# Two-layer kernel: the experts of layer 1 on plain fp32 matmuls, their product moved from VectorE to GpSimd

## What is computed

```python
logits = einsum('bsd,ed->bse', xn, gate_w)            # 16 experts
topk_w, topk_idx = top_k(softmax(logits).transpose, cap)   # cap = 512 tokens per expert and batch
x_tok = take(xn, topk_idx)
g = einsum('becd,efd->becf', x_tok, Wg)               # 256 -> 512
u = einsum('becd,efd->becf', x_tok, Wu)
h = gelu(g) * u
eo = einsum('becf,edf->becd', h, Wd) * topk_w         # 512 -> 256, scattered back and added
out = scatter_add(eo) + shared_expert(xn)             # the same three products, for every token
```

## Time and profile before

| | us |
|---|---|
| runs | 4758.56, 4765.51, 4766.25 |
| median | 4765.51 |
| span of the profiled execution | 4756.4 |
| PE busy | 4083.1 (86%) |
| DVE busy | 3477.4 (73%) |
| POOL busy | 2589.5 (54%) |
| ACT busy | 2579.2 (54%) |

### The profile page before, as it was taken

One profiled execution on the slowest core, in us unless ns is written; L12 is line 12 of the kernel. 1 busy time (PEld: TensorE's weight loads), 2 busy tenths in 40 slices (PEclk: granted clock), 3 DMA queues, 4 the chain that ended last, 5 costly groups with the idle time before them and its releaser, 6 DMA issues. The chain is left out here.

```text
span 4756.4 us, 68001 instructions
## 1 busy us (share of the span) xinstructions
PE 4083.1 (86%) x24660; PEld 3380.9 (71%) x24660; DVE 3477.4 (73%) x4975; ACT 2579.2 (54%) x4869; POOL 2589.5 (54%) x1858
## 2 busy tenths in 40 slices
PE   8899999979999999978888866778888887888865
PEld 7788888858788888867777755656676666666653
DVE  5466666655566666626888889988888888888887
ACT  6544444437444444447576653256667666666655
POOL 3122222223122210026666656878999899999887
PEclk9999999989999999979999967889999999999996
DMA  2022222221122210024444431255655556556658
GB/s 90 19 97 76 85 86 76 88 87 41 52 89 73 88 58 20 22 68 141 148 143 140 141 112 60 81 173 167 192 178 179 176 186 188 173 172 190 188 164 315
DMA packets 271490, 572.90 MB, mean 120 GB/s; under 512 B 37169, under 2 KB 157746, under 8 KB 271154
## 3 DMA queue, kind: packets, MB, share of 16 engines
q1 hardware_dynamic: 246578, 534.98, 33.7%
q0 software_dynamic: 24576, 33.57, 3.9%
HBM read 445.64 MB, written 122.81 MB: 120 GB/s over the span
## 5 line engine op out<-in xcount | busy, mean ns | idle before, releaser
L1595 POOL TENSOR_TENSOR scan_drive_sb<-scan_b_wide_sb,scan_du_sb 128x1024 f32<-128x1024 f32 x512 | 1299.8, 2565 | 269.5 <-DVE scan_h_sb L1507 262.6
L1507 DVE TENSOR_TENSOR_SCAN scan_h_sb<-decay_bank,scan_state_sb,scan_drive_sb 128x512 f32<-128x512 f32 x896 | 1116.2, 1268 | 114.7 <-ACT decay_bank L1845 108.8
L1845 ACT ACTIVATE decay_bank<-scan_delta_sb,a_neg_sb 128x512 f32<-128x512 f32 x1024 | 701.0, 687 | 382.1 <-DVE scan_h_sb L1507 378.9
L1012 PE MATMUL ybank<-v_low_hi_lo_sb,pt_hi_b_sb 128*128 128x384 f32 x2048 | 665.6, 359 | 26.9 <-DVE pt_lo_b_sb L884 20.8
L1514 DVE TENSOR_TENSOR scan_ch_sb<-c_pair,scan_h_sb 128x1024 f32<-128x1024 f32 x512 | 614.2, 1200 | 63.6 <-PE c_pair L1682 63.3
L884 DVE TENSOR_TENSOR pt_lo_b_sb<-pt,pt_hi_b_sb 128x512 fp32r<-128x512 f32 x512 | 352.7, 690 | 420.1 <-ACT pt_hi_b_sb L1058 420.1
L1693 PE MATMUL y_bank<-identity_sb,scan_ch_sb 128*128 128x128 f32 x4096 | 652.2, 291 | 5.1 <-ACT scan_temp_sb L1863 5.1
L1693 PEld LDWEIGHTS y_bank<-identity_sb,scan_ch_sb 128*128 128x128 f32 x4096 | 546.2, 152 | 118.4 <-issue 19.1
L1682 PE MATMUL c_pair<-scan_cc_sb,select_state_sb 128*128 128x512 f32 x1024 | 387.1, 462 | 259.7 <-DVE scan_ch_sb L1514 259.0
L1049 ACT ACTIVATE p_b_sb<-scores,softmax_cols_b_sb 128x1024 f32<-128x1024 f32 x256 | 286.0, 1117 | 546.3 <-DVE softmax_cols_b_sb L878 409.1
L1013 PE MATMUL ybank<-v_low_hi_lo_sb,pt_lo_b_sb 128*128 128x256 f32 x2048 | 573.7, 280 | 0.0
(11 more groups left out here) (328 smaller groups left out, 9898.6 us busy)
## 6 DMA issues: line engine op xcount, KB each, us to landing
scan_b_wide_sb<-b_scratch SPq DMA_DIRECT2D x512, 512.0 KB, 3.9
w_hi_scratch<-split_hi_sb SPq DMA_DIRECT2D x51, 512.0 KB, 2.8
w_lo_scratch<-split_lo_sb SPq DMA_DIRECT2D x51, 512.0 KB, 4.1
expert_hi_sb<-w_hi_scratch SPq DMA_DIRECT2D x48, 512.0 KB, 5.4
expert_lo_sb<-w_lo_scratch SPq DMA_DIRECT2D x48, 512.0 KB, 6.4
x_b_sb<-x SPq DMA_DIRECT2D x16, 512.0 KB, 4.0
split_raw_sb<-WgT SPq DMA_DIRECT2D x16, 512.0 KB, 5.5
x_res_b_sb<-x SPq DMA_DIRECT2D x64, 128.0 KB, 4.9
```

Of the source, the lines that this page charges most:

```text
L1012: e.matmul(k.y_bank[:, 0:D + P], k.pt_hi[n % 2][:, cols], kv.v[:, block, :], start=(kb == 0), stop=False, skip_group_check=True)
L1507: e.tensor_tensor_scan(k.h[i % H_BUFFERS][:, j, :], k.decay_banks[S % DECAY_BANKS][:, :], k.drive[i % DRIVE_BUFFERS][:, j, :], start, ALU. ...
L1595: e.tensor_tensor(k.drive[i % DRIVE_BUFFERS][:, :, :], k.b_wide[i % B_BUFFERS][:, :, :], k.du[c % 2][:, :].unsqueeze(1).broadcast_to([P, P ...
L1845: e.activation(k.decay_banks[S % DECAY_BANKS][:, :], k.delta[c % 2][:, :], ACT.Exp, scale=wt.a[:, n:n + 1]).then_inc(k.s_decay, 1)
```

## The change

The experts' halves go. Tokens, weights and the hidden product are kept as plain fp32, and each product of PE is one fp32 matmul in place of three fp32r ones (the compiler issues an fp32 matmul as two instructions). The split of the weights during attention, its buffers, semaphores and the two DRAM copies go; SP loads the raw weights into six slots of one tile each. The up bank is now copied out by ACT, and GpSimd multiplies the copy with gelu.

```diff
-LOGITS_AT = 13
+LOGITS_AT = 12
-FETCH_AT = (0, 4, 19)
+FETCH_AT = (0, 4, 8)
+W_SLOTS = 6
...
 def attention_gpsimd(e, w, k, consts, b):
-    def split(r, half):
...
-        e.tensor_scalar(hi, raw, 1.0, 0.0, ALU.mult, ALU.add).then_inc(k.s_split, 1)
-        w.wait_ge(k.s_split, 4 * r + 2 * half + 1)
-        e.tensor_tensor(lo, raw, f32(hi), ALU.subtract).then_inc(k.s_split, 1)
...
 def moe_sync(...):
...
-        for half, slot in enumerate((k.w_hi[r % 4], k.w_lo[r % 4])):
-            e.dma_start(f32(slot[:, :]), w_dram[half][r]).then_inc(k.s_w[r % 4], 16)
+        e.dma_start(k.expert_w(r), raw_weight(a, r)).then_inc(k.s_w[r % W_SLOTS], 16)
...
 def moe_scalar(e, w, k, fills, pace, last):
-        e.activation(k.xt_hi[q % 2][:, c, :], fills.bank("moe_turned", q, c), ACT.Copy).then_inc(k.s_xt_hi, 1)
+        e.activation(k.xt[q % 2][:, c, :], fills.bank("moe_turned", q, c), ACT.Copy).then_inc(fills.emptied("moe_turned", q, c), 1)
...
-    def upper(q, f):
-        fills.wait_emptied(w, "moe_up", q, f)
-        if q > 0:
-            wait_down(w, fills, q - 1)
-        e.activation(k.h_hi[:, f, :], k.g[f][:, :], ACT.Copy).then_inc(k.s_h_hi, 1)
+    def up(q, f):
+        fills.wait_filled(w, "moe_up", q, f)
+        w.wait_ge(k.s_h, HB * (q - 1) + f + 1)
+        e.activation(k.u[f][:, :], fills.bank("moe_up", q, f), ACT.Copy).then_inc(fills.emptied("moe_up", q, f), 1)
...
-        c, f, h = part(TURN_AT, s - 1), part(GATE_AT, s - 1), part(UP_AT, s - 2)
+        c, f, h = part(TURN_AT, s - 1), part(GATE_AT, s - 1), part(UP_AT, s - 1)
...
 def moe_gpsimd(e, w, k, fills, consts, pace, xn_dram, acc_dram, last):
-    def lower(q, f):
-        w.wait_ge(k.s_h_hi, HB * q + f + 1)
...
-        e.tensor_tensor(k.h_lo[:, f, :], k.g[f][:, :], f32(k.h_hi[:, f, :]), ALU.subtract).then_inc(k.s_h_lo, 1)
...
+    def product(q, f):
+        fills.wait_emptied(w, "moe_up", q, f)
+        w.wait_ge(k.s_gelu, HB * q + f + 1)
+        if q > 0:
+            wait_down(w, fills, q - 1)
+        e.tensor_tensor(k.h[:, f, :], k.u[f][:, :], k.g[f][:, :], ALU.mult).then_inc(k.s_h, 1)
...
 def moe_vector(e, w, k, fills, consts, pace, last):
-    def turn(q, c):
...
-    def product(q, f):
...
 def moe_tensor(e, w, k, fills, consts, pace):
...
     def up(q, kind, name, f):
...
         for c in range(DC):
-            e.matmul(bank, hi[:, c, cols], xt_hi[:, c, :], start=(c == 0), stop=False)
-            e.matmul(bank, hi[:, c, cols], xt_lo[:, c, :], start=False, stop=False)
-            last = e.matmul(bank, lo[:, c, cols], xt_hi[:, c, :], start=False, stop=(c == DC - 1))
+            last = e.matmul(bank, weight[:, c, cols], k.xt[q % 2][:, c, :], start=(c == 0), stop=(c == DC - 1))
...
     def down(q, j):
...
         for f in range(HB):
-            e.matmul(out, k.h_hi[:, f, rows], hi[:, f, :], start=(f == 0), stop=False)
-            e.matmul(out, k.h_hi[:, f, rows], lo[:, f, :], start=False, stop=False)
-            last = e.matmul(out, k.h_lo[:, f, rows], hi[:, f, :], start=False, stop=(f == HB - 1))
+            last = e.matmul(out, k.h[:, f, rows], weight[:, f, :], start=(f == 0), stop=(f == HB - 1))
```

More of the change, by code:

```diff
@@ L941, in residual @@
         yield
-        for half in range(2 if t < WEIGHTS else 0):
-            split(t, half)
         yield
@@ L2252, in block @@
         if h is not None:
-            upper(q, h)
+            up(q, h)
     def shared(q, s):
@@ L2338, in scatter, with block @@
                              k.out[pair][:, j % 2, :], None, compute_op=ALU.add).then_inc(k.s_scatter[pair], 16)
[L2340 to L2345 removed]
+    def block(q, s):
+        f = part(UP_AT, s - 2)
+        if f is not None:
+            product(q, f)
     def routed(q, s):
[L2348 removed]
+        j = part(DOWN_AT, s - 3)
         if s < SLOT_TILES:
             gather(q - ALL_GROUPS, s)
[L2351 to L2352 removed]
+        block(q, s)
         if j is not None:
             scatter(q, j)
[L2356 removed]
+    yield from moe_order(pace, prepare_steps(), block, choose(), routed, last)
 def moe_vector(e, w, k, fills, consts, pace, last):
[L2360 to L2365 removed]
     def gate_max(q):
@@ L2471, in choose @@
         yield
-    def block(q, s):
-        c, f = part(TURN_AT, s - 2), part(UP_AT, s - 1)
-        if c is not None:
-            turn(q, c)
-        if f is not None:
-            product(q, f)
     def shared(q, s):
-        block(q, s)
         if s == LOGITS_AT + 1:
@@ L2485, in shared @@
             gate_recip(q)
-    yield from moe_order(pace, prepare_steps(), shared, choose(), block, last)
+    yield from moe_order(pace, prepare_steps(), shared, choose(), nothing, last)
 def moe_tensor(e, w, k, fills, consts, pace):
@@ L2514, in logits @@
             for c in range(DC):
-                e.matmul(out, xt_hi[:, c, rows], k.gate_hi[:, c, :], start=(c == 0), stop=False)
-                e.matmul(out, xt_hi[:, c, rows], k.gate_lo[:, c, :], start=False, stop=False)
-                last = e.matmul(out, xt_lo[:, c, rows], k.gate_hi[:, c, :], start=False, stop=(c == DC - 1))
+                last = e.matmul(out, k.xt[q % 2][:, c, rows], k.gate_raw[:, c, :], start=(c == 0), stop=(c == DC - 1))
         last.then_inc(fills.filled("logits", q), 1)
@@ L2531, in up @@
         wait_turned(q)
-        hi, lo = weights(q, kind)
-        xt_hi, xt_lo = k.xt_hi[q % 2], k.xt_lo[q % 2]
+        weight = weights(q, kind)
         cols = slice(f * P, (f + 1) * P)
```

116 lines of the change are left out of this document (25 added, 91 removed).

## The result

The changed kernel takes **4694.69 us** (median, 4690.84 to 4699.42), the kernel before 4762.69 (4758.56 to 4766.25) beside it: ratio 0.9863, 95% interval 0.9849 to 0.9877. By the ratio it is 65 us faster, outside what a measurement can take for no change. The forecast was 4743: the result lies inside the range given (4688 to 4805), near its lower end, but the promised gain was 22 us and the chip gave three times as much. The profiled execution has a span of 4697.7 us against 4756.4, so 58.7 us are there to be found.

A forecast was written before the change was run, and what follows sets the result against it. No single bound: POOL, DVE and PE were nearly full in routed blocks, PE and DVE in shared ones. Attention -11, routed -19, shared +8 gave -22 us against the 4765.5 median: 4743 us, range 4688 to 4805.

The forecast's parts named there:

- the sum for a shared block: Layer 1's 16 shared blocks: PE +2.2 us against 5.8 idle, DVE -4.05; taken as +0.5 each, +8 us in all.
- the routed block: Layer 1's 32 routed blocks: four pieces of a block together -0.6 us, -19 us in all, bounds -72 to +54.
- 8 to 15: Routed block, counted by DVE's scans: three ups, two DVE subtractions; 18.8 us to shrink to 16.5, -2.3.
- 16 to 0: Routed block, an up and three gates, 7.25 us: PE is full and gets four dearer fills, +1.1 us.
- 1 to 3: Routed block, last gate, gelus, two downs, 10.3 us: PE's 0.7 more partly fits its idle time, +0.4 us.
- 4 to 7: Routed block, two downs and a transpose, 8.4 us: +0.2 us.
- attention: Attention stage: the weight split goes, 0.22 us for each of 51 tiles, -11 us, bounds -15 to -7.
- the prices of single instructions: Layer 1: fp32 records 0.43 and 0.216 us; GpSimd's product costs what its subtraction did; ACT's copies 0; weight loads unchanged.
- rival 4: Expert weight loads: fp32 loads take twice 199 ns and are exposed, +283 us, about 5026 us; chance 0.02.
- Rival 1: Expert blocks, steps 16 to 3: PE becomes the bound, +1.7 us per routed, +2.2 per shared block, 4844 us; chance 0.20.
- Rival 2: Routed blocks: DVE's relief removes all coupling and POOL's floor is reached, -72 us, with attention 4683 us; chance 0.18.
- Rival 3: Expert blocks: relief and cost cancel, only attention's gain is left, 4754 us; chance 0.12.

The follow-up runs named there:

- e6: e1 with each expert product made by three fp32r matmuls of the same high halves, low halves left out; 4664.79 us, ratio 0.9803.
- e1: Changed kernel with attention's split of 51 weights and its DRAM writes put back, halves unread; 4721.64 us, ratio 0.9911.
- e3: Changed kernel with turned and up banks given back by a one-column DVE copy behind ACT's copy; 4731.51 us, ratio 0.9938.
- e7: e1 with each expert product made by one fp32r matmul, low halves left out; 4595.00 us, ratio 0.9655.
- e8: Changed kernel with GpSimd multiplying only 64 of 512 columns of gelu and up from the second block on; 4653.97 us, ratio 0.9781.
- e4: Changed kernel with DVE multiplying gelu and up straight from the PSUM bank, without ACT's copy and GpSimd's product; 4716.37 us, ratio 0.9911.
- e9: Changed kernel with all four gelu-up products of a routed block on DVE, from ACT's SBUF copies; 4826.0 us, ratio 1.0144.
- e11: Changed kernel with only the last of four gelu-up products of a routed block on DVE, from SBUF copies; 4698.84 us, ratio 0.9873.

## Why the prediction was wrong

**Failed: the sum for a shared block.** "PE gets +2.2 against 5.8 idle, DVE loses 4.05 ... I take +0.5" was +8 us for 16 blocks; measured are -24.7 for 13 of them and -2.5 in the piece with the other three, so this sum holds 35 of the 37 us by which the forecast missed. The prediction had looked up the waits of the routed stretch only the earlier trace rows and called the shared one by its busy shares. There PE waited 41.8 of its 86.1 idle us for DVE's read-out. The +0.5 is +3.1 for the form of the matmuls, -0.9 for the logits and so -1.7 for DVE's relief. In runs, for each of the 13 blocks: all but the form is worth (619.2 - 572.7) / 13 = 3.6 us (e6 against before, with the logits and whatever the clock did), where the forecast had 2.6; the form costs 23.5 / 13 = 1.8 (e6 against e1), where it had 3.1. I had charged PE's cost in full and credited too little of the relief, and both errors point the same way. The two DVE parts put back singly gave 31 and 11 us, 42 of these 46.5.

**Right, in part by luck: the routed block.** -0.6 us forecast, -15.2 / 32 = -0.5 measured. Cut at the same scans of DVE in both traces (31 blocks of the routed stretch, one every 19 scans, us per block), the pieces are:

| steps | before | after | difference | forecast |
|---|---|---|---|---|
| 8 to 15 | 18.92 | 16.66 | -2.3 | -2.3 |
| 16 to 0 | 7.85 | 9.23 | +1.4 | +1.1 |
| 1 to 3 | 9.24 | 10.10 | +0.9 | +0.4 |
| 4 to 7 | 9.18 | 8.72 | -0.5 | +0.2 |

Eight blocks after, to be read beside the earlier trace rows (the first three pieces, per block 16.2, 8.8 and 11.0 us for 18.8, 7.25 and 10.3):

```profile
sum 129.40, PE 111.77 PEld 68.27 DVE 120.22 ACT 76.58 POOL 126.12; mean PE 13.97 PEld 8.53 DVE 15.03 ACT 9.57 POOL 15.77
sum 70.20, PE 67.45 PEld 38.95 DVE 60.90 ACT 39.91 POOL 68.84; mean PE 8.43 PEld 4.87 DVE 7.61 ACT 4.99 POOL 8.60
sum 87.80, PE 78.79 PEld 58.04 DVE 50.89 ACT 71.82 POOL 78.87; mean PE 9.85 PEld 7.26 DVE 6.36 ACT 8.98 POOL 9.86
```

A cut one scan earlier or later moves a piece's difference by up to 1 us, so the sizes are rough: steps 8 to 15 lose 1.3 to 2.5 us, steps 16 to 3 together gain 1.7 to 2.2. The directions are as forecast, but for steps 4 to 7. The reasons are not all the forecast's: of what steps 16 to 3 gained, the form is 0.9 to 1.2 us (e1 against e6, cut the same way), the rest stands in e6 too, where the forecast gave all its 1.5 to the form. Over a whole block the relief gave 35.7 us / 32 = 1.1 (e6 against before) and the form took 22.6 / 32 = 0.7 (e6 against e1), while PE's records cost 2.7 us of its own time (forecast 3.1). The load and the bank path of DVE put back singly cost 24 and 19 us here, more than the 35.7 together, so they don't simply add.

**Right in mechanism, too small: attention.** -11 forecast; measured 14.4 to tile 63 in these two traces, 17.1 from tile 0 on, 20 to 22 in e1. The mis-sized term is "0.22 us for each of 51 tiles": it fits tiles 34 to 50 (25.93 to 25.71 us), but the last tile of the first sequence alone is shorter by 6.4 us.

**Right: the prices of single instructions.** A gate or up fill is four records with 0.42 us from start to start, a down eight at 0.21 (PE in order of time, after; the last record of each is shown with its full length, in the groups 0.606 and 0.394 us in the mean: (1.88 - 0.606) / 3 and (1.89 - 0.394) / 7):

```profile
3815.97 1.88 PE L2455 MATMUL layer_bank<-moe_xt_sb,expert_sb 128*128 128x512 f32 x4
3818.12 1.89 PE L2464 MATMUL layer_bank<-expert_sb,moe_h_sb 128*128 128x256 f32 x8
```

GpSimd's product is 1276 ns in the shared blocks, as the subtraction was 1301. In the routed ones its spans, 1638 ns in the mean, overlap their followers, as the prediction read them; from start to start it is 1.23 us there too (after):

```profile
3806.93 1.84 POOL L2260 TENSOR_TENSOR moe_h_sb<-moe_u_sb,moe_g_sb 128x512 f32<-128x512 f32 x1
3808.16 2.93 POOL L1559 TENSOR_TENSOR scan_drive_sb<-scan_b_wide_sb,scan_du_sb 128x1024 f32<-128x1024 f32 x1
```

ACT's busy time in both stretches fell by 3 and 13 us. The fp32 weight loads of 128 columns last 196 ns where the fp32r ones took 199, so rival 4 fell:

```profile
L2464 PEld LDWEIGHTS layer_bank<-expert_sb,moe_h_sb 128*128 128x128 f32 x1024 | 190.7, 196 | 65.1 <-ACT moe_out_sb L2191 27.9 <-DVE scan_yt_lo_sb L1424 4.6 <-issue 3.1
```

The Trainium skill ("TensorE: Matmul & The Clock Gate", section "Weight-path perf modes") has fast weight load on for 128 weights of a type other than FP32. The prediction's 0.40 us took the fp32r loads for fast ones, and its "the trace disagrees" says too much: the rows print both kinds as f32 and show that they last the same, not whether either is fast.

**The rivals.** Rival 1 (PE the bound, slower) had PE's dearer records right, as e6 shows, but priced them at 1.7 us per routed and 2.2 per shared block, where the form cost 0.7 and 1.8, and missed that the relief is larger. Rival 2 gave 4683, near the result, for a reason that does not hold: the change took only 10.9 us off POOL's busy time in the routed stretch, POOL idles 128.2 us of it against 132.5, and the largest part of the gain lies in the shared blocks, where POOL is 69% busy. Rival 3 (only attention left) fell.

What stays open: how much of e3's 34 us PE lost at the banks and how much behind DVE's stops, which the same edit brings; why attention's split costs 6.4 us at one tile; and whether the rise of the clock in the shared blocks (0.93 to 0.97) is a gain of its own or follows from PE's shorter waits. No run here holds the one and moves the other.

A version that beats both and computes the same was not found. e6 and e7 are faster but leave the low halves out, e8 most columns of the product. A mixed form (halves for gate and up, fp32 for down) was not run.

## What to carry to other kernels

With several engines 80 to 90% busy none is "the bound": each microsecond of busy time has a rate of exchange, and it differs by stretch. Here, per us of busy time taken off or put on: DVE 0.7 (31 of 43) in the shared blocks and 0.2 in the routed ones; PE 0.5 and 0.3 (e6), less when much is taken (e7: 0.4 and 0.2); POOL 0.05 and 0.3. And a bank that comes free only behind a nearly full engine costs more than the instruction that frees it (e3). So look up the waits of every stretch that the change touches, not of the longest alone, and price relief and cost by the same rate. Before moving an elementwise operation to DVE, look where its operands lie and what GpSimd does then: one operand in PSUM was worth 1.2 us per instruction.

## What the runs showed of the hardware

- A DVE product of 128x512 takes 677 ns with one operand in PSUM and 1848 ns in the mean with both in SBUF beside a busy GpSimd (e4, e9), 5.25 us behind two drives in a row. In e11, with one such product a block, DVE's busy time in the routed stretch rose by 81 us (1230.5 against 1149.2) and the stretch by 4: standing counts as busy, and where nobody waits it is free.
- GpSimd's own product with both operands in SBUF takes 1.23 us from start to start in the shared and in the routed blocks, though the profile's spans there have two lengths (42 of the 124 under 1.4 us, the other 82 over 1.5): most of those 82 reach some 0.6 us into the next instruction. A mean of spans, 1638 ns here, is not what the instruction costs.
- An fp32 record of 512 columns takes 0.42 us from start to start and one of 256 columns 0.21, two records for a product; three fp32r matmuls in their place cost PE 2.7 to 3.4 us less per block of eight gate or up fills and four downs (e6 against e1).
- Single fp32r matmuls (e7) had the clock granted at 0.89 and 0.85 in the two stretches, with PE busy 74% and 69%; the changed kernel, with PE busy 92% and 89%, had 0.97 and 0.96. How much of e7's gain this took, no run here separates.
